# Moving the projections of the next head from the first to the second half of a query pair

## The reference

```python
q, k, v = heads(x @ Wq), heads(x @ Wk), heads(x @ Wv)     # 16 heads, 2048 x 64
sim = q @ k.T * 64 ** -0.5
G = sigmoid(sim)
P = minimum(reversed_cumsum(G), 63)                        # position, counted from the right
sim = sim + interpolate(q @ pos_emb, P)                    # between floor(P) and ceil(P)
attn = softmax(sim)
out = (attn @ v).reshape(2048, 1024) @ Wout + b_out
```

## Time and profile before

| | |
|---|---|
| time, median of 3 runs | 2495.25 us (2495.07 to 2500.59) |
| the profiled execution: its own time, its span | 2493.37 us, 2491.5 us |
| PE busy | 2340.9 us, 94% |
| DVE busy | 1814.7 us, 73% |
| ACT busy | 1745.9 us, 70% |
| POOL busy | 253.6 us, 10% |
| granted TensorE clock, mean over the span | 0.991 |

### The profile page before, as it was taken

The page is one execution under the profiler, slowest core; times in us unless marked ns, Lnnn a source line. Parts: engine busy times, 40 slices in busy tenths (PEclk is TensorE's granted clock), DMA queues, the critical chain, the costliest instruction groups (busy, mean ns, idle before and its releaser), DMA issues. The chain is left out here.

```text
span 2491.5 us, 64093 instructions
## 1 busy us (share of the span) xinstructions
PE 2340.9 (94%) x18687; PEld 1674.2 (67%) x18687; DVE 1814.7 (73%) x4542; ACT 1745.9 (70%) x3767; POOL 253.6 (10%) x417
## 2 busy tenths in 40 slices
PE   7999999999999999999999999999999989999997
PEld 5666666666666666666666666666666656777776
DVE  5888887888888888888888888888888812323231
ACT  5777777777777777777777777777777743444442
POOL 0000000000000000000000000000100001111111
PEclk9999999999999999999999999999999989999998
DMA  2010101010101010101010101010101020101000
GB/s 70 23 38 22 37 21 34 22 38 21 35 22 38 21 35 22 38 21 35 22 38 21 35 22 38 21 37 22 30 13 53 12 63 32 38 25 38 25 27 7
DMA packets 108087, 75.47 MB, mean 30 GB/s; under 512 B 26894, under 2 KB 103823, under 8 KB 107984
## 3 DMA queue, kind: packets, MB, share of 16 engines
q1 hardware_dynamic: 107984, 73.88, 10.8%
HBM read 14.26 MB, written 2.10 MB: 7 GB/s over the span
## 5 line engine op out<-in xcount | busy, mean ns | idle before, releaser
L463 ACT ACTIVATE probsT<-rings 128x512 f32<-128x512 f32 x1024 | 556.4, 595 | 334.9 <-PE rings L615 334.9
L796 DVE TENSOR_REDUCE mx<-Sc 128x1 f32<-128x1024 f32 x512 | 626.8, 1224 | 130.2 <-PE Sc L607 115.1
L615 PEld LDWEIGHTS rings<-ident,probs 128*128 128x128 f32 x4096 | 434.3, 141 | 269.0 <-issue 194.2
L615 PE MATMUL rings<-ident,probs 128*128 128x128 f32 x4096 | 572.9, 283 | 22.1 <-ACT probs L484 1.2
L607 PE MATMUL Sc<-qk,q_now 64*128 64x512 f32 x2048 | 529.6, 615 | 46.8 <-ACT probs L484 26.5
L484 ACT ACTIVATE probs<-Sc,nbias 128x1024 f32<-128x1024 f32 x512 | 566.9, 1121 | 8.6 <-DVE nbias L813 8.6
L629 PE MATMUL out<-probsT,V_now 128*64 128x128 f32 x8192 | 530.0, 277 | 0.0
L629 PEld LDWEIGHTS out<-probsT,V_now 128*64 128x64 f32 x8192 | 439.5, 137 | 58.9 <-issue 45.5
L773 DVE COPY_PREDICATED z<-mask,z 128x224 f32<-128x224 int16 (+5 forms) x768 | 390.8, 509 | 107.6 <-DVE cut L763 33.0
L607 PEld LDWEIGHTS Sc<-qk,q_now 64*128 64x128 f32 x2048 | 188.1, 187 | 232.5 <-issue 231.5
L374 POOL TENSOR_TENSOR prod<-cut,z 128x350 f32<-128x350 f32 x128 | 120.2, 939 | 1577.5 <-DVE z L785 1577.5
(11 more groups left out here) (121 smaller groups left out, 2507.1 us busy)
## 6 DMA issues: line engine op xcount, KB each, us to landing
q_now<-qk SPq DMA_DIRECT2D x256, 64.0 KB, 2.0
xv<-xT SPq DMA_DIRECT2D x113, 128.0 KB, 2.2
q_far<-qk SPq DMA_DIRECT2D x256, 32.0 KB, 1.8
V_now<-V SPq DMA_DIRECT2D x16, 512.0 KB, 3.0
at<-attn SPq DMA_DIRECT2D x16, 512.0 KB, 3.2
probs<-in_x_dram SPq DMA_DIRECT2D x4, 512.0 KB, 5.5
wqk<-in_L_attn_Wq_dram SPq DMA_DIRECT2D x32, 64.0 KB, 2.1
xin<-in_x_dram SPq DMA_DIRECT2D x16, 128.0 KB, 2.8
```

What stands on the lines that cost most here:

```text
L463: nc.scalar.activation(probsT[:, u, 4 * s:4 * s + 4, :], ring[k % 2][:, :].rearrange("p (t q) -> p t q", q=P), ACT.Copy).then_inc(slot_out, 1)
L615: last = nc.tensor.transpose(ring[k % 2][:, j * P:(j + 1) * P], probs[:, u, (4 * s + j) * P:(4 * s + j + 1) * P], ident[:, :])
L796: nc.vector.tensor_reduce(mx[:, u, half:half + 1], Sc[:, half * HALF:(half + 1) * HALF], AX.X, ALU.max).then_inc(dve_unit, 1)
```

## The change

`project` and `project_values` move on TensorE from the first half of a pair to the second, behind the transposes of unit 0 and ahead of its outputs. The outputs of the last unit then run in one stretch. Their slots are renumbered to match (q and k 8, V 9, the transposes of unit 0 4 to 7), in pairs with and without projections alike. ScalarE empties the slots of q, k and V between the two halves of the exponentials of unit 1 and does the last `scale` after them. SP's program keeps its order; the number that `load_tile` waits for follows `Slots().values`, and `load_near` gets a wait for the keys of the pair before.

```diff
 class Slots:
-    def __init__(self, proj=True):
+    def __init__(self):
         self.last = [0, 1, 2, 3]
-        self.qk, self.values = 4, 5
-        at = 6 if proj else 4
-        self.now = [at, at + 1, at + 2, at + 3]
+        self.now = [4, 5, 6, 7]
+        self.qk, self.values = 8, 9
...
     # block.sync, body
                 if near:
+                    wait_apart(sp, slot_out, base - 1, waited)
                     load_near(g // PAIRS + 1)
...
     # block.scalar
-            def exps(g, u):
-                act.wait_ge(bias_ready, g * 2 + u + 1)
-                for half in range(2):
-                    cols = slice(half * 2 * BANK, (half + 1) * 2 * BANK)
-                    nc.scalar.activation(probs[:, u, cols], Sc[:, cols], ACT.Exp, bias=nbias[:, u:u + 1],
-                                         accum_out=sums[:, u, half:half + 1]).then_inc(exp_done, 1)
+            def exp_half(g, u, half):
+                if half == 0:
+                    act.wait_ge(bias_ready, g * 2 + u + 1)
+                cols = slice(half * 2 * BANK, (half + 1) * 2 * BANK)
+                nc.scalar.activation(probs[:, u, cols], Sc[:, cols], ACT.Exp, bias=nbias[:, u:u + 1],
+                                     accum_out=sums[:, u, half:half + 1]).then_inc(exp_done, 1)
...
                     scale(g - 1, 0)
-                exps(g, 0)
-                if proj:
-                    project(g + PAIRS, not odd, base, at.qk, alone=not val)
-                if val:
-                    values(g, base, at.values)
+                exp_half(g, 0, 0)
+                exp_half(g, 0, 1)
...
                 transposed(0, base, at.now)
+                exp_half(g, 1, 0)
+                if proj:
+                    project(g + PAIRS, not odd, base, at.qk, alone=not val)
+                if val:
+                    values(g, base, at.values)
+                exp_half(g, 1, 1)
                 if not first:
                     scale(g - 1, 1)
-                exps(g, 1)
...
     # block.tensor, body
                     transposes_and_turn(g - 1, 1, base, at.last, 0, evicted=not second)
-                    outputs(g - 1, 1, base, at.last, tiles=range(FIRST))
-                if proj:
-                    weights_at = (g // PAIRS) * 64 + 128 if val else H * 64 - 16
-                    project(g + PAIRS, not odd, base, at.qk, weights_at, alone=not val)
-                if val:
-                    project_values(g + PAIRS, base, at.values)
-                if not first:
-                    outputs(g - 1, 1, base, at.last, tiles=range(FIRST, NT))
+                    outputs(g - 1, 1, base, at.last)
                 if far:
                     wait_apart(pe, slot_out, base + at.now[0], waited)
                     window(g + 2, par if far_par is None else far_par)
...
                 transposes_and_turn(g - 1, 0, base, at.now, 1, first)
+                if proj:
+                    weights_at = (g // PAIRS) * 64 + 128 if val else H * 64 - 16
+                    project(g + PAIRS, not odd, base, at.qk, weights_at, alone=not val)
+                if val:
+                    project_values(g + PAIRS, base, at.values)
                 outputs(g, 0, base, at.now, empty=not first)
```

More of the change, by code:

```diff
@@ L456, in _, with transposed @@
                     steps(1)
-            def transposed(u, base, slots):
-                for s in range(4):
+            def transposed(u, base, slots, sets=range(4)):
+                for s in sets:
                     k = slots[s]
@@ L478, in empty_halves @@
                 nc.scalar.activation(halves[:, u, :], out[:, 0:P], ACT.Copy).then_inc(halves_out, 1)
-            def exps(g, u):
-                act.wait_ge(bias_ready, g * 2 + u + 1)
-                for half in range(2):
-                    cols = slice(half * 2 * BANK, (half + 1) * 2 * BANK)
-                    nc.scalar.activation(probs[:, u, cols], Sc[:, cols], ACT.Exp, bias=nbias[:, u:u + 1],
-                                         accum_out=sums[:, u, half:half + 1]).then_inc(exp_done, 1)
+            def exp_half(g, u, half):
[4 more added lines that the diff above has]
+                                     accum_out=sums[:, u, half:half + 1]).then_inc(exp_done, 1)
             def body(g, odd, late=False, first=False, proj=True, val=True, far=True, near=True):
                 base = slots_before(g, late)
-                at = Slots(proj)
+                at = Slots()
                 if near:
@@ L528, in _ @@
             body(G - 1, True, late=True, proj=False, val=False, far=False, near=False)
-            base, at = slots_before(G, True), Slots(proj=False)
+            base, at = slots_before(G, True), Slots()
             empty_halves(G - 1, 0)
```

## The result

The changed kernel takes 2690.16 us (median of 4 runs, 2686.64 to 2697.28) where the kernel before takes 2495.16 in the same comparison: a ratio of 1.0782, 95% interval [1.0759, 1.0806]. The forecast was 2634, range 2564 to 2707, so the sign and the range were right and the size was 56 us short. The profiled execution has a span of 2691.0 us at a mean granted clock of 0.984.

The account below looks back on a forecast made before the run. TensorE's order was taken to bound the 112 pairs with V projections; late `q_now` would lengthen pairs from 15.40 to 16.74 us: 107 x 1.34 = +143, less 3 in pairs 112 to 119, from 2493.4 to 2634 us, range 2564 to 2707.

Parts of the forecast that it names:

- the transfers get in each other's way: Rival: `q_now` follows `xv` at once and every landing takes 2.9 us; +2.24 us a pair, 2730 us; chance 5%.
- The sum: Over the whole run: 107 pair steps each 1.34 us longer, +143 us; five loop restarts counted as unchanged.
- the period of an undisturbed pair: Time from one pair's logits to the next: 12.31 us until V begins plus 4.43 us to the next logits, 16.74 us.
- TensorE's start after the landing: Between the landing of `q_now` and the next logits on TensorE: 0.04 us.
- The first half: From the pair's start until the V projection begins on TensorE: 12.31 us.
- the ring's wait: The projection, behind four transposes in a ring of two banks, starts 0.28 us late; it could be nothing.
- The gap ahead of `q_now`: On SP, from the end of issuing `xv` to the next issue: 0.34 us, bounded by nothing and 0.70.
- Its upper bound: Top of the range, 2707 us: +2.00 us a pair, allowing a `q_now` gap of 0.70 and 0.3 for late landing.
- The case of a fall in every pair: Rival: TensorE's rests drop the clock to 1.2 GHz, +14.1 us on 107 pairs, about 4000 us; chance 1%.
- `load_near`'s wait: SP's new wait once in a head, for keys projected in the pair before: claimed to cost nothing.
- ScalarE's order: Emptying q, k and V between unit 1's exponentials: hidden by the DMA wait; with early `q_now`, logits held about 1 us.
- The rival of a hidden transfer: `q_now` arrives by 14.82 us, so TensorE's own order binds and the kernel gets faster, about 2428 us; chance 6%.

Follow-up runs that it names:

- the kernels of 6: Wait for exponentials, then needless matmuls, ahead of the `q_now` wait: twelve or seven in the changed kernel, 2798.92 and 2703.12 us; twelve with `xv` loaded twice, 2818.33 us.
- the kernel of 5: The changed kernel with `xv` loaded twice, the second time into a buffer that nothing reads: 2859.72 us, ratio 1.1473.
- 1: The changed kernel with SP's load of `q_now` put ahead of the load of `xv` and its wait: 2444.56 us, ratio 0.9794.
- 7: The changed kernel with `q_now` loaded ahead of `xv`, plus four tiles of unit 0's outputs between its transposes and the projections: 2431.84 us, ratio 0.9753.

## Why the prediction was right, and what it under-sized

**The mechanism is shown, from both sides.** The late wait put alone into the old kernel makes the loss (1.0897); taken out of the changed kernel, by order or by a second buffer, it leaves a gain (0.979). That the new order on TensorE and ScalarE costs time by itself has fallen: it is worth 50 us as soon as `q_now` doesn't stand behind `xv`. That the transfers get in each other's way has fallen too: `q_now` lands in 2.0 us in the median, as forecast, and with a second `xv` ahead of it no later.

**The sum.** In the profiled executions pair 112 starts at 1976.99 us, against 1774.60 before: +202.4 where the sum said +143. It comes apart like this: the 100 ordinary pairs 100 x (17.22 - 15.39) = +183; the pairs just behind the five restarts +15 together; the restart pairs themselves -2; the first two pairs +7. Of the difference of 59 from the forecast, to a rounding,

- 33 are the period of an undisturbed pair, 17.07 instead of 16.74, on 100 pairs. The failed term is TensorE's start after the landing: I took 0.04 us from a single matmul in the earlier trace rows, and 0.23 was measured, +0.2. In the trace nothing runs between that landing and that matmul. Ahead of the logits stands a second wait, for exponentials long done, whose instructions (L67, L68) run only when the queries are there, at 1075.4 and 1075.5 in the pair shown; where the kernels of 6 have it earlier, the logits start 0.06 us after the landing. TensorE's rest is hardly the reason, since in the earlier trace rows it had rested 1.68 us, too. The first half took 12.43 instead of 12.31: the ring's wait is 0.34, I had 0.28, and the rest of the first half is 0.06 longer. The gap ahead of `q_now` was 0.21 in one body and 0.55 in the other, 0.38 on average for my 0.34. Issue of `xv`, distance of the two `q_now` issues and landing were as put.
- 15 are in two kinds of ordinary pairs: some 11 in the seven with slow logits, some 5 in the six in which every second head begins, where the first `q_now` issue takes up to 1.65 us (1.25 at 604.94) instead of 0.49.
- 8 are what the pairs behind the restarts cost beyond the forecast: in four of these five the logits take 3.1 to 3.4 us. The mean clock gives a like size for all slow logits together: 0.016 x 2691 = 43 us lost, against 0.009 x 2491 = 22.
- 5 are the first two pairs, of which the second has slow logits, too (3.27 us), less 2 gained at the restarts, which I had counted as unchanged.

That the range held is in part luck. Its upper bound was made of the gap ahead of `q_now` and of late landings, and these two came as put; the terms that did grow, the start after the landing and the clock, were not in it.

**The clock was the step that failed in its reasoning.** I wrote that the rows speak against a fall, from a single rest. The trace of before has another restart, which I overlooked, where the logits of 407.31 follow 3.49 us of rest. TensorE's timeline of the kernel before, and the stretch table there:

```profile
407.31 3.64 PE L607 MATMUL Sc<-qk,q_now 64*128 64x512 f32 x8 [3.49 <-issue]
```

```profile
407.31:410.90 3.59, 3.59 (x9) 1.27 (x9) 1.48 (x2) 0.00 (x0) 0.00 (x0) 0.53 0.02 5
```

There the clock did fall. The case of a fall in every pair (about 4000 us) did not come, but between "never" and "always" lay what happened: one pair in ten, up to 1.7 us each in its logits. The Trainium skill ("TensorE: Matmul & The Clock Gate", HAM oscillation) describes a loop of about 2 us of matmuls and a DMA wait of 3 to 5 us, in which every turn starts at half rate. This kernel has much more work between its rests, and the runs agree only in part: 12 of 112 pairs with rests of 2.0 to 3.45 us, 60 of 100 ordinary pairs with rests near 3 us in the kernel of 5; and in the stretch shown the clock is back at 1.00 as soon as the logits are done.

**What was hidden as said.** The last eight projecting pairs gave back 4 us (forecast 3): most of them follow each other at 14.73 us. `load_near`'s wait and ScalarE's order cost nothing in the changed kernel: pair 33, which has the wait, lasts 16.93 us, and TensorE's logits wait for exponentials in six places only. Where `q_now` is early, as in 1 and 7, the second exponential does hold the logits, but 0.1 to 0.4 us instead of the 1 us foreseen. TensorE's share is 86% instead of "near 89%", and its wait for `q_now` 253 us instead of 200.

**The rival of a hidden transfer**, 2428 us, is the kernel that one gets after mending SP: 2445 with the order alone, 2424 with two more shifts. Its price for TensorE's own order (14.82 us a pair, measured 14.92) was right; only the condition for it wasn't met.

## What to carry to other kernels

When a step moves on one engine, list the queues whose waits count that step and ask what stands behind each wait; the program of such a queue has to be reordered along with it, so that a transfer wanted soon isn't behind one that can't start yet. Price the path from the releasing instruction to the waiting one from a pair of rows in which the same engine waits for the same kind of transfer, not from one start, and count the waits that the program puts between the two: one that was met long ago may still cost time behind one that is met last. And a rest on the busiest engine may cost its clock as well: look at every rest of that length in the trace, not at one.

## What was not expected of the hardware

After rests of 2.0 to 3.45 us the granted clock fell in some pairs and not in others (12 of 112), and the same rest of 2.37 us was followed by logits of 1.99 us at 1058.69 and of 2.48 at 1612.38; what decides isn't shown. TensorE started 0.23 us after the landing with a second, long met wait behind the first, and 0.06 after without it; what part of that the needless matmuls had, which came in with the same edit, no run separates. Seven more matmuls in each body lengthened the pair with a loop restart from about 18.1 to 23.7 us.
